# Two feed-forward networks around an attention layer: last tiles scaled and quantised on other engines, value bias row made from sums

## The chip, the cores and the metric

The kernel runs on one core of one Trainium2 chip. A core has a matmul engine (TensorE, PE in the profile; its weight loads are PEld), VectorE (DVE), ScalarE (ACT), GpSimd (POOL) and SyncE (SP), which here only issues DMAs. They run side by side and wait for one another by semaphores. The metric is the device time of one execution in microseconds; the median of three executions is given. Times within the trace are counted from the span's start.

## The reference

x has 2 sequences of 2048 rows of 256 values, 4096 rows in all. Cut to what matters:

```python
x = x + 0.5 * ffn(layernorm(x), w_gate, w_up, w_down)
x = x + attn(layernorm(x), Wq, bq, Wk, bk, Wv, bv, Wo, bo)   # biases bq, bk, bv, bo
x = x + 0.5 * ffn(layernorm(x), w_gate, w_up, w_down)

def fp4_quant_dequant(x):          # blocks of 16 values along a row
    scale = max(max(abs(xb)) / 6.0, 1e-12)
    q = GRID[searchsorted(MID, abs(xb / scale))] * sign(xb / scale) * scale
def fp4_linear(x, w): return fp4_quant_dequant(x) @ fp4_quant_dequant(w).T
def ffn(x, w_gate, w_up, w_down):  # 256 -> 704 -> 256
    h = silu(fp4_linear(x, w_gate)) * fp4_linear(x, w_up)
    return fp4_linear(h, w_down)
def attn(x, ...):                  # one head over all 2048 rows of a sequence
    w = softmax((qr @ kr.T + qi @ ki.T) / sqrt(256))
    return interleave(w @ vr, w @ vi) @ Wo.T + bo
```

## The kernel before, in words

The 4096 rows are 32 tiles of 128 rows, numbered 0 to 31 (NT is 32). Each network goes over the tiles in steps; f is 0 for the first network and 1 for the second. Every engine has its own program, written out by hand, and its order is the order of the code: within a queue nothing overtakes. All matmuls of the networks are done in halves of precision, an upper part (T_hi, w_hi) and a lower part (T_lo, w_lo), so that three products make one.

What happens to the hidden values of a tile k, in order:
- TensorE makes gate and up products into `gu` (a PSUM region); ScalarE applies silu; VectorE multiplies to `z` (L854).
- VectorE takes the maximum of each block (`amax`, L867), and the scales `s_up`, `s_neg` and their inverse `s_inv` (to L880). `z` times `s_inv` is `y` (L908 on VectorE, L607 on GpSimd); ScalarE makes the absolute values (L1495, for the last tile L1486); VectorE rounds to the grid in two operations (`rounded` L889, `grid` L895); grid times `s_neg` is `zq` (L625 on GpSimd, 704 columns and then 64; for the last two tiles L974 and L976 on VectorE).
- TensorE transposes `zq` into PSUM (L1887, six or eight passes). ScalarE copies the upper part `T_hi` (L1513; for the last two tiles in two pieces, L1519 and L1520). The lower part comes from VectorE by a subtraction (L950), for tile 29 from a product with the negative identity on TensorE (`chain_lower`, L2045) and a copy by ScalarE (`T_lo`, L1527), for the last two from VectorE (L960 to L966).
- TensorE projects down into the one bank `dn` (ten passes of L2017 and seven of L2024; for the last two tiles L2172 and L2181; tile 31 has a bank of its own, `dn_last`). ScalarE copies `dn` out to `down` (`down_out`, L1502), and GpSimd adds that to `x` (`residual`, L592). TensorE may start the next tile's projection only when the copy is done: it waits for `down_done`.

In step c the engines work at tiles c-1 to c+3 at once. The step functions decide by comparisons of c with NT what differs for the last tiles: NT-4 is 28, NT-3 is 29, NT-2 is 30, NT-1 is 31. Tiles 30 and 31 are projected in `last_two`. ScalarE also takes the statistics of finished tiles (`mean_of`, `minus_mean`, `variance_of`; st_junk in the rows) in the first network.

Behind the first network come keys, queries and scores. The bias of keys and values is turned into two rows, `rk_sum` and `bv_sum`, by products of four pieces each (L1894): the bias spread over 128 columns (`bkB`, `bvB`) against `wq_s` and the transposed output weights `woT`. ScalarE copies both rows out (`bias_rows`), GpSimd adds `bo` (`output_bias`), and ScalarE takes the first scores out of PSUM after that. Early in the run, GpSimd makes `wv_d`, differences of the value weights.

## Time and profile before

| | us |
|---|---|
| median of 3 runs | 896.74 (896.65 to 897.13) |
| the profiled execution | 896.82 |
| its span, first to last instruction | 895.0 |
| TensorE busy | 873.4 (98%) |
| VectorE, ScalarE, GpSimd busy | 710.1, 627.5, 566.9 |
| share of the chain that ended last | TensorE 90%, VectorE 3%, ScalarE 3% |

The granted TensorE clock is printed as full throughout. Busy time of a matmul includes its way through the array, so passes overlap in the rows; the distance between two starts is what a pass costs in the queue. The first network ends near 258 us, the attention near 690 us, and the last 15 us are the end of the second network.

### The profile page before, as it was taken

Reading aid. Unit: us, or ns where it says so; the run is one execution under the profiler, and the core shown is the slowest. Engines: PE = TensorE matmul, PEld = TensorE weight load, DVE = VectorE, ACT = ScalarE, POOL = GpSimd, SP = SyncE. Lnnn points to the kernel's source line nnn. Section 1 sums busy time; section 2 is a strip of 40 time slices with the busy share of each in tenths; the row PEclk is TensorE's granted clock in tenths of the full one; section 3 lists DMA queues with packets and bytes.
Section 4 is the critical chain, followed back from the end, with each engine's and each line's share of the span. In section 5 each row is a group of like instructions: output and inputs, shape, how many; then the busy total and the mean of one; then the engine's idle time right before and its main releaser. Section 6 shows DMA issues by size and latency. Waiting matters only on the chain.

```text
span 895.0 us, 14668 instructions
## 1 busy us (share of the span) xinstructions
PE 873.4 (98%) x4842; PEld 754.2 (84%) x4842; DVE 710.1 (79%) x1104; ACT 627.5 (70%) x1395; POOL 566.9 (63%) x636
## 2 busy tenths in 40 slices
PE   4999999999999999999999999999999999999997
PEld 3788999999988788888888788888778999999996
DVE  7987999999977897855656646455688999999997
ACT  6789888977685866758685786758785676555543
POOL 5577889988520554536658454636667778877762
PEclk9999999999999999999999999999999999999999
DMA  9200000000000000000000000000000000000001
GB/s 314 72 1 1 1 1 2 0 2 1 1 1 1 1 1 1 0 1 0 1 1 1 1 1 1 0 1 1 1 1 1 1 25 25 24 25 25 1 25 48
DMA packets 11948, 13.73 MB, mean 15 GB/s; under 512 B 864, under 2 KB 11104, under 8 KB 11872
## 3 DMA queue, kind: packets, MB, share of 16 engines
q1 hardware_dynamic: 11872, 12.79, 4.3%
q8 instruction: 39, 0.64, 0.3%
q14 instruction: 37, 0.30, 0.1%
HBM read 8.59 MB, written 4.19 MB: 14 GB/s over the span
## 4 chain that ended last, share of the span: by engine, by line
PE 90%; DVE 3%; ACT 3%; issue 1%; POOL 1%; DMA 1%; SPq 0%; DVEq 0%; ACTq 0%; POOLq 0%
PE bank L2006 26%; PE bank L2270 19%; PE bank L2333 18%; PE bank_b L2017 7%; PE bank L1887 7%; PE bank_b L2024 5%; PE bank L2260 2%; PE bank L2078 1%; PE bank_b L2078 1%; DMA wk_s<-in_L_attn_Wk 1%; PE bank L1894 1%; PE bank L1883 1%; POOL xt L713 1%; DVE rounded L889 0%; PE bank_b L1894 0%
## 5 line engine op out<-in xcount | busy, mean ns | idle before, releaser
L676 POOL TENSOR_TENSOR p_lo<-s_ring,p_hi 128x512 fp32r<-128x512 f32 x128 | 167.7, 1315 | 187.2 <-ACT p_hi L1725 186.8
L2006 PE MATMUL bank<-w_hi,T_hi 128*128 128x512 f32 (+1 forms) x384 | 149.8, 390 | 0.9 <-DVE s_ring L1096 0.7
L625 POOL TENSOR_TENSOR zq<-grid,s_neg 128x256 f32<-128x256 f32 (+2 forms) x184 | 142.1, 800 | 13.6 <-DVE grid L895 13.6
L2006 PE MATMUL bank<-w_lo,T_hi 128*128 128x512 f32 (+1 forms) x384 | 144.0, 375 | 0.0
L2006 PE MATMUL bank<-w_hi,T_lo 128*128 128x512 f32 (+1 forms) x384 | 144.0, 375 | 0.0
L2333 PE MATMUL bank<-p_hi,xv 128*128 128x512 f32 x512 | 140.8, 393 | 0.0
L1072 DVE TENSOR_TENSOR top<-bank,top 128x512 f32<-128x512 f32 x92 | 63.5, 690 | 93.4 <-ACT s_ring L1708 91.7
L1708 ACT ACTIVATE s_ring<-bank 128x512 f32<-128x512 f32 x128 | 75.8, 593 | 73.3 <-PE bank L2270 66.7
L1513 ACT ACTIVATE T_hi<-bank 128x1024 fp32r<-128x1024 f32 (+1 forms) x68 | 64.7, 951 | 80.1 <-PE bank L1887 80.0
L2333 PEld LDWEIGHTS bank<-p_hi,xv 128*128 128x128 f32 x512 | 94.0, 188 | 18.1 <-DVE p_lo L1054 0.2
L607 POOL TENSOR_TENSOR y<-z,s_inv 128x960 f32<-128x960 f32 (+1 forms) x56 | 99.7, 1781 | 5.4 <-DVE rounded L889 4.6
L2270 PE MATMUL bank<-q_hi,k_hi 128*128 128x512 f32 x256 | 100.6, 393 | 0.5 <-ACT s_ring L1708 0.3
L2270 PE MATMUL bank<-q_hi,k_lo 128*128 128x512 f32 x256 | 99.7, 389 | 0.0
L2270 PE MATMUL bank<-q_lo,k_hi 128*128 128x512 f32 x256 | 99.6, 389 | 0.0
L1714 ACT ACTIVATE s_ring<-s_ring 128x512 f32<-128x512 f32 x128 | 79.2, 622 | 20.5 <-DVE s_ring L1096 20.5
L1096 DVE TENSOR_TENSOR s_ring<-s_ring,bank 128x512 f32<-128x512 f32 x128 | 84.6, 677 | 0.4
L867 DVE TENSOR_REDUCE amax<-z 128x60 f32<-128x960 f32 (+2 forms) x72 | 74.9, 1040 | 11.7 <-ACT z L1547 9.0
L1725 ACT ACTIVATE p_hi<-s_ring 128x512 fp32r<-128x512 f32 x128 | 80.7, 631 | 4.4 <-PE bank L2333 1.2
L2006 PEld LDWEIGHTS bank<-w_hi,T_lo 128*128 128x128 f32 x384 | 72.1, 188 | 11.8
L2006 PEld LDWEIGHTS bank<-w_hi,T_hi 128*128 128x128 f32 x384 | 72.2, 188 | 11.6 <-DVE s_ring L1096 1.1
L2333 PE MATMUL bank<-p_lo,xv 128*128 128x512 f32 x256 | 80.8, 390 | 0.0
L2017 PE MATMUL bank_b<-wd_hl,T_hi 128*128 128x256 f32 x600 | 79.9, 279 | 0.0
(238 smaller groups left out, 1925.4 us busy)
## 6 DMA issues: line engine op xcount, KB each, us to landing
out<-x SPq DMA_DIRECT2D x7, 512.0 KB, 2.9
x<-in_L_attn_hidden_states SPq DMA_DIRECT2D x3, 1024.0 KB, 12.3
x<-in_L_attn_hidden_states SPq DMA_DIRECT2D x2, 512.0 KB, 7.5
wraw<-in_L_ffn_w_down SPq DMA_DIRECT2D x1, 704.0 KB, 7.6
wraw<-in_L_ffn_w_up SPq DMA_DIRECT2D x1, 640.0 KB, 5.4
wq_s<-in_L_attn_Wq SPq DMA_DIRECT2D x1, 512.0 KB, 7.0
wk_s<-in_L_attn_Wk SPq DMA_DIRECT2D x1, 512.0 KB, 7.9
wo_s<-in_L_attn_Wo SPq DMA_DIRECT2D x1, 512.0 KB, 8.4
```

The lines of the kernel that those rows point to most:

```text
L607: nc.gpsimd.tensor_tensor(out=blocks(y[:, lo:Z]), in0=blocks(z[:, lo:Z]), in1=spread(s_inv[:, lo // BLOCK:ZB], (Z - lo) // BLOCK), op=ALU. ...
L625: last = nc.gpsimd.tensor_tensor(out=blocks(zq[:, to:to + hi - lo]), in0=blocks(grid[:, lo:hi]), in1=spread(s_neg[:, par, lo // BLOCK:hi / ...
L676: nc.gpsimd.tensor_tensor(out=lower_buf(n, c), in0=score_buf(n, c), in1=upper_buf(n, c).bitcast(F32), op=ALU.subtract).then_inc(plo_done, 1)
L867: nc.vector.tensor_reduce(out=amax[:, n], in_=blocks(z[:, lo:hi]), axis=AX_X, op=ALU.max, apply_absolute_value=True).then_inc(amax_done, 1)
L1096: nc.vector.tensor_tensor(out=p, in0=p, in1=shift_bank, op=ALU.subtract).then_inc(diff_done, 1)
L1708: nc.scalar.activation(score_buf(n, c), score_bank(c), ACT.Copy).then_inc(evac_done, 1)
L1714: nc.scalar.activation(p, p, ACT.Exp, scale=SCALE).then_inc(exp_done, 1)
L1725: nc.scalar.activation(upper_buf(n, c), score_buf(n, c), ACT.Copy).then_inc(phi_done, 1)
L2006: last = nc.tensor.matmul(gu[:, lo:hi], lhsT=T[:, par, HK + kd, :], rhs=w[:, kd, lo:hi], start=n == 0, stop=n == len(terms) - 1)
L2017: nc.tensor.matmul(dn, lhsT=T_hi[:, par, k, :], rhs=wd_hl[:, k, half:half + D], start=n == 0, stop=False)
L2270: last = nc.tensor.matmul(score_bank(c), lhsT=kk[:, kd, t], rhs=q[:, kd, :], start=kd == 0 and i == 0, stop=kd == KD - 1 and i == 2, skip_ ...
L2333: last = nc.tensor.matmul(sum_bank[:, kd, :], lhsT=xv[:, c, of], rhs=p, start=c == 0 and first == 0, stop=c == CH - 1 and first == 2, skip ...
```

## The change

It reorders the last steps of both networks and makes the value bias row in another way:
- GpSimd scales tile 31 (`scaled_last`, in place in `z`) where VectorE did, and quantises tile 30 where VectorE did. VectorE goes from tile 30's grid straight to tile 31, with other buffers (`gu` for the absolute values, `yabs_sb` for the result, `bank5` for its transposes).
- GpSimd adds tiles 28 and 29 to x only after tile 31 is quantised.
- ScalarE copies tile 28 out of `dn` after the absolute values of tile 31, and tile 29 between the two pieces of tile 30's upper part.
- In the second network TensorE transposes tile 29 between the passes of tile 28; in both, tile 31 between those of tile 30.
- The value bias row: GpSimd multiplies `woT` by the bias and adds the four pieces in two steps; TensorE makes one product with ones, after the first score product. ScalarE copies the key row out in step 30 and the value row later.
- The statistics of tiles 28 and 29 go from the first network to the first rounds of attention.

The core of the diff:

```diff
-        dn_last = bank4[:, 1, 0:D]
+        dn_last = bank4[:, 2, 0:D]
...
-            return bank5[:, 0:2, :] if k == NT - 2 else bank2[:]
+            return bank5[:, 0:2, :] if last(k) else bank2[:]
+
+        def quantised_of(k):
+
+            return yabs_sb if last(k) else zq
...
-                nc.gpsimd.tensor_copy(bkB[:], b3[:, 1, :].unsqueeze(2).to_broadcast([P, KE, P]))
-                nc.gpsimd.tensor_copy(bvB[:],
-                                      b3[:, 2, :].unsqueeze(2).to_broadcast([P, KE, P])).then_inc(aw["bcast"], 1)
+                nc.gpsimd.memset(ones[:], 1.0).then_inc(aw["ones"], 1)
+                nc.gpsimd.tensor_copy(bkB[:],
+                                      b3[:, 1, :].unsqueeze(2).to_broadcast([P, KE, P])).then_inc(aw["bcast"], 1)
+
+            def value_bias_sums():
+
+                pool.wait_ge(aw["nv"], KD)
+                nc.gpsimd.tensor_tensor(out=woT[:], in0=woT[:], in1=b3[:, 2, :].unsqueeze(2).to_broadcast([P, KE, D]),
+                                        op=ALU.mult).then_inc(aw["bv_mul"], 1)
+                pool.wait_ge(aw["bv_mul"], 1)
+                nc.gpsimd.tensor_tensor(out=woT[:, 0:2, :], in0=woT[:, 0:2, :], in1=woT[:, 2:4, :],
+                                        op=ALU.add).then_inc(aw["bv_add"], 1)
+                pool.wait_ge(aw["bv_add"], 1)
+                nc.gpsimd.tensor_tensor(out=woT[:, 0, :], in0=woT[:, 0, :], in1=woT[:, 1, :],
+                                        op=ALU.add).then_inc(aw["bv_sum"], 1)
...
+                def scaled_last():
+
+                    pool.wait_ge(inv_done, number(f, NT - 1))
+                    nc.gpsimd.tensor_tensor(out=blocks(z[:, 0:I]), in0=blocks(z[:, 0:I]), in1=spread(s_inv[:, 0:HB], HB),
+                                            op=ALU.mult).then_inc(y_done, 1)
+
                 def step(c, par):
                     if whole(f, c + 2):
                         pool.wait_ge(inv_done, number(f, c + 2))
                         negative_scales(c + 2, par)
-                    if hidden(c - 1) and c < NT:
+                    if hidden(c - 1) and c < NT - 3:
                         residual(c - 1, 1 - par)
                     if hidden(c + 2) and ahead(c + 2):
                         scaled_by_pool(c + 2)
-                    if chain(c + 1) and not late(c + 1):
+                    if c == NT - 3:
+                        scaled_last()
+                    if chain(c + 1) and not last(c + 1):
                         quantised(c + 1, 1 - par)
+                    if c == NT - 2:
+                        pool.wait_ge(zq_done, number(f, NT - 1))
+                        residual(NT - 4, 0)
+                        residual(NT - 3, 1)
+                    if c == NT - 1:
+                        residual(NT - 2, 0)
...
                     if f == 0 and c == NT:
+                        value_bias_sums()
                         output_bias()
...
-                    abs_k = silu[:] if last(k) else yabs_of(f, k, lo, hi)
+                    abs_k = gu[:, 0:I] if last(k) else yabs_of(f, k, lo, hi)
...
-                        scaled(NT - 1)
                         to_grid(NT - 2)
-                        quantised_late(NT - 2, 1 - par)
...
-                def quantised_late(k, par):
-
+                def quantised_last(par):
+
+                    k = NT - 1
                     dve.wait_ge(grid_done, number(f, k))
-                    dve.wait_ge(T_done, number(f, k - 1))
-                    nc.vector.tensor_tensor(out=blocks(zq[:, 0:I]), in0=blocks(grid[:, 0:I]),
+                    dve.wait_ge(zq_done, number(f, k) - 1)
+                    nc.vector.tensor_tensor(out=blocks(yabs_sb[:, 0:I]), in0=blocks(rounded[:, 0:I]),
                                             in1=spread(s_neg[:, par, 0:HB], HB), op=ALU.mult)
...
                     if late(c) and chain(c):
                         late_upper(c, par)
+                        if c == NT - 2:
+                            down_out(c - 1, 1 - par)
+                        late_upper_rest(c, par)
                     if extra and c == NT - 1:
                         keys_upper(0, 0)
-                    if hidden(c - 1) and c < NT and c != NT - 2:
+                    if hidden(c - 1) and c < NT and c not in (NT - 3, NT - 2):
...
-                    if extra and c == NT - 3:
+                    if c == NT - 3:
                         absolute(NT - 1)
+                        down_out(c - 1, 1 - par)
+                    if extra and c == NT - 2:
+                        key_bias_out()
...
-            bias_rows()
             sum_inputs_upper(0, 0)
+            value_bias_out()
...
-                    if n == 1 and c in (4, 7):
-                        statistics(NT - 2 + (c - 4) // 3, NT - 2 + (c - 4) // 3)
+                    if n == 1 and c in (4, 7, 10, 13):
+                        statistics(NT - 4 + (c - 4) // 3, NT - 4 + (c - 4) // 3)
...
-                product(bv_sum, bvB, woT, False).then_inc(aw["rows"], 1)
+                pe.wait_ge(aw["ones"], 1)
+                pe.wait_ge(aw["bv_sum"], 1)
+                pe.wait_ge(x_last, 1)
+                nc.tensor.matmul(bv_sum, lhsT=ones[:], rhs=woT[:, 0, :], start=True, stop=True,
+                                 skip_group_check=True).then_inc(aw["rows"], 1)
...
-                        project_down_first(par, dn)
-                        wait_lowered(f, c)
+                        if f and c == NT - 4:
+                            project_down_first(par, dn, 0, 2)
+                            wait_lowered(f, c)
+                            transpose_chain(f, c + 1)
+                            project_down_first(par, dn, 2)
+                            chain_lower(f, c + 1, 1 - par)
+                        else:
+                            project_down_first(par, dn)
+                            wait_lowered(f, c)
                         project_down_rest(par, dn)
...
                         transpose_keys(0, 0)
-                    down_late(0, dn)
+                    pe.wait_ge(down_done, (NT - 1) * f + NT - 2)
+                    down_late(0, dn, 0, 2)
                     transpose_chain(f, NT - 1)
+                    down_late(0, dn, 2, HK)
                     down_late_rest(0, dn)
-                    down_late(1, dn_last)
+                    if f == 0:
+                        pe.wait_ge(aw["rows_s"], 1)
+                    down_late(1, dn_last, 0, HK)
                     down_late_rest(1, dn_last)
 
-                def down_late(par, dn):
-
-                    pe.wait_ge(late_hi, 2 * f + par + 1)
-                    if par == 0:
...
             queries(0)
             transpose_keys(0, 1)
+            scores(0, 0)
             value_bias_row()
-            scores(0, 0)
+            scores(0, 1)
             pe.wait_ge(aw["rows_s"], 2)
             transpose_keys(0, 2)
-            scores(0, 1)
             pe.wait_ge(klo_done, 2)
...
```

What the order of instructions shows at three places. First ScalarE in the first network, from step 29 to the statistics behind it; `bank<-y` is absolute values of tile 30, `down` is the copy out of `dn`. Before:

```order
L1495 ACTIVATE bank<-y 128x704
L1502 ACTIVATE down<-bank_b 128x256
L1413 ACTIVATE st_junk,total<-x 128x256
L1513 ACTIVATE T_hi<-bank 128x1024
L1419 ACTIVATE nmean<-total 128x1
L1420 ACTIVATE nmean_s<-total 128x1
L1527 ACTIVATE T_lo<-bank 128x896
L1529 ACTIVATE T_hi<-bank 64x128
L1486 ACTIVATE silu<-z 128x704
L1426 ACTIVATE st_junk,var<-x,nmean_s 128x256
L1447 ACTIVATE xk<-x,nmr,rstd 128x256
L1502 ACTIVATE down<-bank_b 128x256
```

In the changed kernel (its lines are numbered anew: L1539 is `down_out`, L1523 the absolute values of tile 31, L1556 and L1561 the two pieces of the upper part):

```order
L1532 ACTIVATE bank<-y 128x704
L1450 ACTIVATE st_junk,total<-x 128x256
L1550 ACTIVATE T_hi<-bank 128x1024
L1456 ACTIVATE nmean<-total 128x1
L1457 ACTIVATE nmean_s<-total 128x1
L1568 ACTIVATE T_lo<-bank 128x896
L1570 ACTIVATE T_hi<-bank 64x128
L1523 ACTIVATE bank<-z 128x704
L1539 ACTIVATE down<-bank_b 128x256
L1463 ACTIVATE st_junk,var<-x,nmean_s 128x256
L1484 ACTIVATE xk<-x,nmr,rstd 128x256
L1556 ACTIVATE T_hi<-bank 128x512
```

The copy of tile 28 (`down`) moves from the second row to behind `T_lo` and the absolute values of tile 31, and stands in both networks at this place; the copy of tile 29 moves between the pieces of tile 30's upper part.

Then TensorE at the end of the second network, from the down projection of tile 28 on. Before:

```order
L2006 MATMUL bank<-w_hi,T_lo 128x384
L2017 MATMUL bank_b<-wd_hl,T_hi 128x256 x10
L2024 MATMUL bank_b<-wd_hl,T_hi 128x256 x2
L2024 MATMUL bank_b<-wd_hl,T_lo 128x256 x5
L1887 MATMUL bank<-ident,zq 128x128 x6
L2045 MATMUL bank<-T_hi,neg_ident 128x512 x2
L2017 MATMUL bank_b<-wd_hl,T_hi 128x256 x10
L2024 MATMUL bank_b<-wd_hl,T_hi 128x256 x2
L2024 MATMUL bank_b<-wd_hl,T_lo 128x256 x5
L1887 MATMUL bank<-ident,zq 128x128 x6
L2172 MATMUL bank_b<-wd_hl,T_hi 128x256 x10
```

In the changed kernel (L2066 and L2073 are the ten and seven passes, L1932 the transposes, L2094 the product with the negative identity):

```order
L2055 MATMUL bank<-w_hi,T_lo 128x384
L2066 MATMUL bank_b<-wd_hl,T_hi 128x256 x4
L1932 MATMUL bank<-ident,zq 128x128 x6
L2066 MATMUL bank_b<-wd_hl,T_hi 128x256 x6
L2094 MATMUL bank<-T_hi,neg_ident 128x512 x2
L2073 MATMUL bank_b<-wd_hl,T_hi 128x256 x2
L2073 MATMUL bank_b<-wd_hl,T_lo 128x256 x5
L2066 MATMUL bank_b<-wd_hl,T_hi 128x256 x10
L2073 MATMUL bank_b<-wd_hl,T_hi 128x256 x2
L2073 MATMUL bank_b<-wd_hl,T_lo 128x256 x5
L1932 MATMUL bank<-ident,zq 128x128 x6
L2232 MATMUL bank_b<-wd_hl,T_hi 128x256 x4
```

The six transposes of tile 29 and the product behind them move ahead of the end of tile 28, and tile 31's transposes move up into the first passes of tile 30.

Last GpSimd behind the first network. Before, from the quantising of tile 29:

```order
L625 TENSOR_TENSOR zq<-grid,s_neg 128x704
L625 TENSOR_TENSOR zq<-grid,s_neg 128x64
L592 TENSOR_TENSOR x<-x,down 128x256
L529 TENSOR_TENSOR var<-var,eps_all 128x4
L532 TENSOR_TENSOR rstd<-var,mhalf 128x4
L535 TENSOR_TENSOR nmr<-nmean,rstd 128x4
L592 TENSOR_TENSOR x<-x,down 128x256 x2
L585 TENSOR_TENSOR bias_row<-bias_row,bo_row 128x256
```

In the changed kernel, from the same place (L650 is `scaled_last`):

```order
L642 TENSOR_TENSOR zq<-grid,s_neg 128x704
L642 TENSOR_TENSOR zq<-grid,s_neg 128x64
L650 TENSOR_TENSOR z<-z,s_inv 128x704
L642 TENSOR_TENSOR zq<-grid,s_neg 128x704
L642 TENSOR_TENSOR zq<-grid,s_neg 128x64
L609 TENSOR_TENSOR x<-x,down 128x256 x3
L584 TENSOR_TENSOR woT<-woT,b 128x1024
L587 TENSOR_TENSOR woT<-woT 128x512
L590 TENSOR_TENSOR woT<-woT 128x256
L602 TENSOR_TENSOR bias_row<-bias_row,bo_row 128x256
```

GpSimd scales tile 31 and quantises tile 30, adds three tiles one behind another, and makes three operations on `woT` ahead of the bias sum.

## Rows read from the trace of the kernel before

**Rows 1.** TensorE's waits, whole run: us in total, times, longest.
```profile
PE bank L1894 <- DMA wk_s<-in_L_attn_Wk: 12.8, 1, 12.8
PE bank L2045 <- ACT T_hi L1513: 1.1, 1, 1.1
```

**Rows 2.** TensorE timeline, value bias product: start, us, engine, line.
```profile
262.09 1.89 PE L1894 MATMUL bank<-woT,bvB 128*128 128x256 f32 x8
263.63 0.58 PE L2270 MATMUL bank<-q_hi,k_hi 128*128 128x512 f32 x1
```

**Rows 3.** Groups by line and shape, GpSimd: count, busy us, mean ns.
```profile
L676 POOL TENSOR_TENSOR p_lo<-s_ring,p_hi 128x512 fp32r<-128x512 f32 x128 | 167.7, 1315 | 187.2 <-ACT p_hi L1725 186.8
...
L625 POOL TENSOR_TENSOR zq<-grid,s_neg 128x704 f32<-128x704 f32 x60 | 86.1, 1435 | 5.2 <-DVE grid L895 5.2
L592 POOL TENSOR_TENSOR x<-x,down 128x256 f32<-128x256 f32 x62 | 45.9, 741 | 27.8 <-ACT down L1502 23.8
```

**Rows 4.** Timelines of GpSimd and VectorE near 25 us.
```profile
24.58 0.81 POOL L573 COPY bvB<-b 128x512 f32<-128x512 f32 x1
25.35 1.89 POOL L579 TENSOR_TENSOR wv_d<-wv_s 128x1024 f32<-128x1024 f32 x1
...
26.48 0.83 DVE L798 TENSOR_SCALAR wsm<-wsm 128x88 f32<-128x88 f32 x1
```

**Rows 5.** TensorE timeline, end of the first network.
```profile
248.91 1.33 PE L2017 MATMUL bank_b<-wd_hl,T_hi 128*128 128x256 f32 x10
...
258.38 0.50 PE L2260 MATMUL bank<-k_hi,m_hi 128*128 128x512 f32 x1 [0.25 <-DVE k_lo L1031]
```

**Rows 6.** ScalarE timeline, end of the first network.
```profile
246.27 0.38 ACT L1502 ACTIVATE down<-bank_b 128x256 f32<-128x256 f32 x1 [0.66 <-PE bank_b L2024]
...
249.11 0.92 ACT L1527 ACTIVATE T_lo<-bank 128x896 fp32r<-128x896 f32 x1 [0.97 <-PE bank L2045]
...
250.34 0.79 ACT L1486 ACTIVATE silu<-z 128x704 f32<-128x704 f32 x1
251.04 0.49 ACT L1426 ACTIVATE st_junk<-x,nmean_s 128x256 f32<-128x256 f32 x1
```

**Rows 7.** Chain that ended last, 225 to 270 us: start, us, what.
```profile
244.24 1.17 PE bank_b L2017 x10
245.41 0.82 PE bank_b L2024 x7
246.23 0.66 PE bank L1887 x6
...
261.38 0.87 PE bank L1883 x8
```

**Rows 8.** Waits of all engines, 285 to 345 us.
```profile
ACT s_ring L1708 <- PE bank L2270: 10.5, 14, 0.9
```

**Rows 9.** Chain that ended last, second network's end.
```profile
881.10 1.31 DVE z L908
...
887.48 0.89 DVE zq L974
```

**Rows 10.** TensorE timeline, end of the second network.
```profile
878.28 1.33 PE L2017 MATMUL bank_b<-wd_hl,T_hi 128*128 128x256 f32 x10
...
880.26 0.81 PE L1887 MATMUL bank<-ident,zq 128*128 128x128 f32 x6
...
882.76 1.33 PE L2017 MATMUL bank_b<-wd_hl,T_hi 128*128 128x256 f32 x10
...
890.12 1.44 PE L2172 MATMUL bank<-wd_hl,T_hi 128*128 128x256 f32 x10
```

**Rows 11.** ScalarE timeline, end of the second network.
```profile
880.46 0.38 ACT L1502 ACTIVATE down<-bank_b 128x256 f32<-128x256 f32 x1 [1.61 <-PE bank_b L2024]
...
882.96 0.92 ACT L1527 ACTIVATE T_lo<-bank 128x896 fp32r<-128x896 f32 x1 [0.82 <-PE bank L2045]
```

**Rows 12.** Chain that ended last, first passes of the run.
```profile
12.76 3.75 PE bank L1894 x8
```

64 lines of the change are left out of this document (36 added, 28 removed).

## Prediction, made before the changed kernel ran

> **What bounds the kernel now.** I read the page's busy line first (TensorE is busy 873.4 of 895.0 us, in the table above), then TensorE's waits [rows 1]. After the initial wait for a weight DMA of 12.8 us, no wait is longer than the 1.1 us near the very end. So TensorE sets the time nearly everywhere. The change can gain in two ways only: by fewer passes on TensorE, or by closing its small gaps. It can lose wherever it makes TensorE wait. Then I read the timelines of all engines around the two ends of the networks (240 to 270 us, 855 to 895 us) and, because one broadcast on GpSimd goes, around 20 to 42 us. A time of the chain and a time of the timeline can differ by up to 0.2 us for the same instructions, since ends of matmuls are modelled; I count intervals between starts.
>
> **Part 1, the value bias product.** Before, four fp32 products show as eight passes that begin at 262.09, and the next score product begins at 263.63 [rows 2]: 1.54 us. One product of the same width is a quarter, 0.39. Gain 1.15 us. It now needs GpSimd's three sums first. Nearest rows [rows 3, 4]: 1024 elements 1.89 us, 512 elements 1.32, 256 elements 0.74, so 4.0 us in all. They start once GpSimd has added tile 30, which I put at 259.6 (below), and end at 263.6. TensorE comes to the product only after the first score product, near 265.4. The 1.8 us between them is the cover. If it were gone, each microsecond of lateness would cost one, since the next score product is queued behind. The same few queue places move ScalarE's copy of the row behind the 1.06 us copy of xv; I see 0.6 us of room there.
>
> **Part 2, the end of the first network.** The accumulator of the down projection is one bank (dn). TensorE may start tile 29's products only when ScalarE has copied tile 28 out. Before, that copy is at 246.27, long ahead of TensorE's start at 248.91 [rows 5, 6]. The order of ScalarE after the change puts it behind T_lo (249.11), the 64-row remainder and the absolute values of tile 31 (250.34) [rows 6]. None of these can move up: T_lo waits for TensorE's subtraction product, which stands behind the key bias product on TensorE. GpSimd's scaling of tile 31, about 1.45 us by the 704-wide form [rows 3], is done by 248.4 and doesn't count. So the copy takes the place in which a statistic ran, 251.04, and with 0.39 us ends at 251.43. TensorE starts tile 29 at about 251.5 instead of 248.91: **2.6 us late**.
>
> How much comes back? From 248.91 to the query product at 258.38 are 9.47 us. Pure work in it: three times 1.17 and 0.82, two sets of six transposes at 0.66, one set of eight at 0.87 [rows 7], together 8.2. The rest, 1.3 us, are gaps. After the change the gaps left are one of 0.2 (the transposes of tile 30 and of the keys end near 255.05, ScalarE then still finishes the upper part, 0.6, and the copy of tile 29, 0.39, at 255.25) and small hand-overs of 0.3. Start of the query product: 251.5 + 8.2 + 0.5 = 260.2, against 258.38: +1.8. The low part of the keys on VectorE is ready near 259.8, so it is not what is waited for any more. GpSimd's last residual follows the copy of tile 30, near 258.8, and ends at 259.6, as used in part 1.
>
> Around the bias row I add 0.1: the first score product now comes straight after the transposes, and its second half has to wait some 0.2 us for the low part of the queries, which the old bias product covered; one change between kinds of products goes. Parts 1 and 2 together: +1.8 - 1.15 + 0.1 = **+0.7**. From there to the second network TensorE runs without a gap that the change touches. The statistics of tiles 28 and 29 move into the first block of scores, where ScalarE stands up to 0.9 us before each copy of a score bank [rows 8]. I put a tile's statistics at 1.2 us of ScalarE, so two rounds hide one tile; without that cover two tiles would cost 2.4 us.
>
> **Part 3, the end of the second network.** Before, the chain runs through VectorE, which scales tile 31 from 881.10 and quantises it until 888.5 [rows 9]. After: scaling goes to GpSimd (881.1 to 882.55), VectorE goes straight on with tile 30's grid (to 882.95), GpSimd quantises tile 30 by about 884.75 (1.44 and a remainder of 0.3), and VectorE is through with tile 31 near 886.35: 2.15 us sooner. But TensorE doesn't get that. Its first four passes of tile 28 start at 878.28, the transposes of 29 then at 878.75 instead of 880.26 [rows 10]. T_lo followed those transposes by 2.70 (882.96) [rows 11], so it starts at 881.45. The absolute values follow 1.23 later as in the first network, at 882.7, the copy of tile 28 0.7 after them at 883.4 [rows 6], and it ends at 883.8. It was at 880.46 before [rows 11]. TensorE has finished tile 28 at 882.05 and stands until 883.8. Tile 29 then starts at 883.85 instead of 882.76 [rows 10]. Tile 29's passes end at 885.85, the transposes of 30 at 886.5; the upper part of 30 and the copy of 29 (0.6 and 0.39) end at 887.6. Four passes 0.5, transposes 0.66, six passes 0.7, seven 0.85: the last group of ten starts at 890.3. Before: 890.12 [rows 10]. So **+0.2**: the gap at tile 30's transposes is closed, and the same time is lost at the bank.
>
> **Part 4, the start.** GpSimd drops a 0.81 us copy and sets ones instead (at most 0.2), so wv_d begins 0.6 sooner [rows 4]. This matters because VectorE's small operation L798, 0.83 us long, ends at 27.31 just when wv_d ends at 27.24 [rows 4]; an operation of a tenth of the elements of the others shouldn't take that long. It seems held by GpSimd, and it lies on the chain that leads to a short gap of TensorE near 36.5. Gain between 0 and 0.5; since the copy of bk now meets another VectorE operation, I take **-0.2**. The Trainium skill's page "SBUF — State Buffer", section "Who interferes with whom", says that VectorE in a two-port mode and GpSimd exclude each other for a whole instruction. By that rule the hold moves with wv_d's end and the gain is near 0.3; by the row alone, without a mechanism, it is 0 and the sum 0.2 higher.
>
> **Sum.** +0.7 + 0.2 - 0.2 = +0.7. The profiled execution of before took 896.82 us (span 895.0 and 1.8 around it), 0.08 above the median of 896.74. So 897.5 for such an execution, and **897.4** for a median.
>
> **Rivals.**
> Stalls at the bank don't bind (faster). If the copy of tile 28 came in time in both networks, the first end would save 1.8 us against my count, and the second 1.9, up to the 2.15 by which VectorE is sooner: 893.7. For it speaks that VectorE was the last chain before [rows 9]. Against it: both orders of ScalarE are fixed, and the copy stands behind two instructions whose inputs are late. It decides if the copy ends before 249 in the first network or before 882 in the second. Only the second of these is thinkable: 895.5. Chance 6%.
> The clock falls in the new gap (slower). After the 12.8 us wait at the start the eight first passes took 3.75 us [rows 12], though eight like them took 1.54 later [rows 2]: that is the level of 1.2 GHz against 2.4. If a gap of 2.6 us is enough, the passes behind it cost about 2.2 us more: 899.6. The longest gap after which this trace shows full speed is 1.1 us [rows 1], so the point from which it decides lies between 1.1 and 12.8. Chance 8%. The Trainium skill's page "TensorE: Matmul & The Clock Gate", section "Part 1: The HAM clock gate (the "warmup" mystery)", tells of a gate that halves the clock when TensorE has been idle; this trace agrees for 12.8 us and doesn't say for 2.6.
> GpSimd's sums come late (slower). If the in-place product with a broadcast operand takes over twice 1.89 us, the cover of 1.8 is gone and the cost is the rest, 0.5 to 2 us: 898 to 899.4. For it: no row has this form in place. Against: wv_d has the same width with a broadcast operand. Chance 6%.
> My forecast, with its sizes: 80%, own range 896.5 to 898.3.
>
> **How the numbers follow.** A measurement of this kernel can tell from no change what is beyond 0.2%, 1.8 us: below 894.9 or above 898.5. Forecast and late sums lie mostly inside. Faster gets the no-stall case and a little of its half: 5%. Slower gets the clock case, part of the late sums and the tail of my sum: 12%. Same: 83%. The range takes in the half case and most of the late sums, from 896.0 to 898.7.
>
> **What would show it.** First network: the copy of tile 28 at about 251 behind the absolute values, tile 29's products at 251.5, a TensorE wait of about 2.5 us on down, the query product near 260. Bias: two passes, 0.4 us, no wait for GpSimd. Second network: a wait of 1.7 us before tile 29's products, VectorE idle before its last lower parts, and an end within 0.5 us of the old one counted from 878.3. Start: L798's follower short, 0.2 us gained by 37. I am wrong if the products of tile 29 start without that wait, if passes behind it last 0.6 instead of 0.38 us, or if the three sums end after 265.

## Result, and the profile after

| | before | changed |
|---|---|---|
| median of 20 executions each | 896.38 us (895.92 to 897.13) | 897.46 us (896.53 to 899.05) |
| ratio, 95% interval | | 1.0013 (1.0007 to 1.0019) |
| profiled execution, its span | 896.82, 895.0 | 897.36, 895.5 |
| TensorE, VectorE, GpSimd busy | 873.4, 710.1, 566.9 | 871.4, 701.6, 575.4 |

The change makes the kernel 0.13% slower: under the 0.2% that the prediction called no change, but more than nothing. The time fell within 0.1 us of the forecast of 897.4. Part of that is luck, as the section on the reasons shows.

TensorE's waits in the changed kernel behind the first DMA (us in total, times, longest), where [rows 1] had nothing over 1.1 us:

```profile
PE bank_b L2066 <- ACT down L1539: 2.3, 1, 2.3
PE bank_b L2066 <- issue: 1.6, 1, 1.6
PE bank_b L2232 <- ACT down L1539: 1.0, 1, 1.0
```

The first row is tile 29 of the first network, the second tile 29 of the second, the third tile 30 of the second. "issue" means that the profile shows nothing that was waited for, but the timeline below does: it is the same copy.

The end of the first network, TensorE's timeline (start, us, engine, line); before: [rows 5].

```profile
246.60 1.89 PE L1939 MATMUL bank<-wq_s,bkB 128*128 128x256 f32 x8
248.14 0.81 PE L2094 MATMUL bank<-T_hi,neg_ident 128*128 128x512 f32 x2
251.29 1.44 PE L2066 MATMUL bank_b<-wd_hl,T_hi 128*128 128x256 f32 x10 [2.35 <-ACT down L1539]
...
252.80 0.75 PE L2073 MATMUL bank_b<-wd_hl,T_lo 128*128 128x256 f32 x5
253.39 0.82 PE L1932 MATMUL bank<-ident,zq 128*128 128x128 f32 x6
...
259.90 0.39 PE L2320 MATMUL bank<-k_hi,m_hi 128*128 128x512 f32 x1
```

ScalarE's timeline at the same place; before: [rows 6].

```profile
248.98 0.92 ACT L1568 ACTIVATE T_lo<-bank 128x896 fp32r<-128x896 f32 x1 [0.98 <-PE bank L2094]
...
250.09 0.74 ACT L1523 ACTIVATE bank<-z 128x704 f32<-128x704 f32 x1
250.86 0.38 ACT L1539 ACTIVATE down<-bank_b 128x256 f32<-128x256 f32 x1
```

Read the two together: `down` ends at 251.24, and the ten passes start at 251.29. The key bias product began at 246.60, 0.12 sooner than before (246.72); the query product begins at 259.90, 1.52 later than before. So this end cost 1.64 us. The last row of TensorE has no wait: the low part of the keys, which TensorE waited for before, is now there in time.

The value bias row: GpSimd's sums, and the product with ones on TensorE; before: [rows 2].

```profile
259.43 1.90 POOL L584 TENSOR_TENSOR woT<-woT,b 128x1024 f32<-128x1024 f32 x1
261.40 1.29 POOL L587 TENSOR_TENSOR woT<-woT 128x512 f32<-128x512 f32 x1
262.78 0.73 POOL L590 TENSOR_TENSOR woT<-woT 128x256 f32<-128x256 f32 x1
```
```profile
265.18 0.59 PE L2013 MATMUL bank<-woT,ones 128*128 128x256 f32 x2
```

The sums end at 263.51, 1.67 before TensorE comes. At the query product the changed kernel is 1.52 late; at the same score products near 268.5 it is 0.41 late. So the value bias row gave 1.11 us. The product itself gave 1.29: its eight passes took 1.54 us before, and the two that are left take 0.25 to the next start. What stands around it took 0.18 back.

The end of the second network, TensorE's timeline; before: [rows 10].

```profile
878.51 0.63 PE L2066 MATMUL bank_b<-wd_hl,T_hi 128*128 128x256 f32 x4
878.99 0.85 PE L1932 MATMUL bank<-ident,zq 128*128 128x128 f32 x6
...
884.08 1.41 PE L2066 MATMUL bank_b<-wd_hl,T_hi 128*128 128x256 f32 x10 [1.58 <-issue]
...
886.15 0.82 PE L1932 MATMUL bank<-ident,zq 128*128 128x128 f32 x6
887.92 0.73 PE L2232 MATMUL bank_b<-wd_hl,T_hi 128*128 128x256 f32 x4 [0.96 <-ACT down L1539]
...
890.67 1.33 PE L2232 MATMUL bank<-wd_hl,T_hi 128*128 128x256 f32 x10
```

ScalarE's copy of tile 28 at the same place:

```profile
883.60 0.39 ACT L1539 ACTIVATE down<-bank_b 128x256 f32<-128x256 f32 x1
```

From the first passes of tile 28 to the last group of ten are 12.16 us; before 11.84. So 0.32 us were lost, although the transposes of tile 29 came 1.50 us sooner, counted from the same first passes.

The start: VectorE's and GpSimd's timelines near 25 us; before: [rows 4].

```profile
26.90 0.25 DVE L831 TENSOR_SCALAR wsm<-wsm 128x88 f32<-128x88 f32 x1
```
```profile
25.02 2.07 POOL L596 TENSOR_TENSOR wv_d<-wv_s 128x1024 f32<-128x1024 f32 x1
```

The small operation that took 0.83 us takes 0.25. Counted against before, TensorE's timeline is 0.32 to 0.36 us late from 20 to 29 us (the first weights landed 0.14 later in this execution) and some 0.15 early from 37 us on, so about 0.5 us came back there.

### The profile page after: what moved, and what is told of

The parts are those of the page before. It is cut to its first block, busy times and chain, and to the rows that moved or that the text cites. A ratio compares the mean times of both kernels' runs of the same rounds, so it can differ in the third digit from the quotient of the medians.

```text
span 895.5 us, 14659 instructions
## 1 busy us (share of the span) xinstructions
PE 871.4 (97%) x4836; PEld 752.9 (84%) x4836; DVE 701.6 (78%) x1098; ACT 626.8 (70%) x1395; POOL 575.4 (64%) x645
## 4 chain that ended last, share of the span: by engine, by line
PE 94%; DVE 2%; ACT 1%; issue 1%; DMA 1%; SPq 0%; POOL 0%; DVEq 0%; POOLq 0%; ACTq 0%
PE bank L2055 27%; PE bank L2330 20%; PE bank L2393 18%; PE bank_b L2066 8%; PE bank L1932 7%; PE bank_b L2073 5%; PE bank L2320 2%; PE bank L2127 1%; PE bank_b L2127 1%; DMA wk_s<-in_L_attn_Wk 1%; PE bank L1928 1%; PE bank L1939 1%; ACT s_ring L1759 0%; PE bank_b L1932 0%; PE bank L2094 0%
## 5 line engine op out<-in xcount | busy, mean ns | idle before, releaser
L642 POOL TENSOR_TENSOR zq<-grid,s_neg 128x64 f32<-128x64 f32 (+2 forms) x188 | 145.3, 800 | 14.3 <-DVE grid L929 14.3
L2066 PE MATMUL bank_b<-wd_hl,T_hi 128*128 128x256 f32 x600 | 80.4, 280 | 3.9 <-ACT down L1539 2.3
L2066 PEld LDWEIGHTS bank_b<-wd_hl,T_hi 128*128 128x128 f32 x600 | 77.5, 188 | 4.5 <-ACT down L1539 2.8
```

Source lines behind the costliest of these rows:

```text
L642: last = nc.gpsimd.tensor_tensor(out=blocks(zq[:, to:to + hi - lo]), in0=blocks(grid[:, lo:hi]), in1=spread(s_neg[:, par, lo // BLOCK:hi / ...
L2066: nc.tensor.matmul(dn, lhsT=T_hi[:, par, k, :], rhs=wd_hl[:, k, half:half + D], start=k == 0 and half == 0, stop=False)
```

## Experiments

Twelve kernels, in four groups. An expectation names its theories by letters, and the text behind it says which of them the run bears out. "Before" stands for the kernel before, run on the same chip in the same group (each group had another chip); it had medians of 896.45 (group of the first four), 896.42 (the next four), 896.82 (the next three) and 897.12 us (the last). Ratios are against it.

### e1_first, e2_second, e3_both: the place of one copy

The copy of tile 28 out of `dn`: in the first network back to its old place (e1), in the second one place up, ahead of the absolute values of tile 31 (e2), or both (e3). Nothing else of the change is touched.

```diff
-                    if hidden(c - 1) and c < NT and c not in (NT - 3, NT - 2):
+                    if hidden(c - 1) and c < NT and c != NT - 2 and (f == 0 or c != NT - 3):
                         down_out(c - 1, 1 - par)
...
                     if c == NT - 3:
+                        if f:
+                            down_out(c - 1, 1 - par)
                         absolute(NT - 1)
-                        down_out(c - 1, 1 - par)
```

(This is e3; e1 has only the effect for f = 0, e2 only that for f = 1.)

Expected of e1_first: 

> The changed kernel, with ScalarE's copy of tile 28 at its old place in the first network only (ahead of the upper part of tile 29). Theory A (the late copy holds the one bank, and TensorE's 2.35 us wait in the first network is real cost): the wait goes, tile 29's products start near 248.9, the query product near 258.2 instead of 259.9; the other waits that come back, tile 31's quantising among them, keep some 0.2 us. Time 1.4 to 1.9 us below the changed kernel, 895.6 to 896.1, about 0.6 us below the kernel before. Theory B (the wait only takes the place of VectorE's or the key chain's, which would be next): less than 0.5 us below the changed kernel, above 897.0.

Expected of e2_second: 

> The changed kernel, with the copy of tile 28 ahead of the absolute values of tile 31 in the second network only. It can't go to its old place there, since the end of tile 28's products now stands behind tile 29's upper part in the queue. Theory A: the copy starts at 882.85 instead of 883.60, tile 29's products at 883.35, and all of it reaches the end: 0.7 us less, 896.8. VectorE gets the absolute values 0.3 us later, which costs nothing, since tile 31 is quantised 1.9 us before its transposes. Theory B (VectorE's chain is what the end hangs on, so a later tile 31 costs): no change or up to 0.3 us more, 897.5 to 897.8.

Expected of e3_both: 

> Both edits of the two runs before. Theory A: the two ends are 600 us apart and their gains add, 2.1 to 2.6 us below the changed kernel: 894.9 to 895.4, faster than the kernel before by 1.0 to 1.5 us. Theory B: within 0.5 us of the changed kernel, not below the kernel before.

Measured: e1 895.35 us (11 executions, ratio 0.9993, 0.9984 to 1.0002); e2 897.52 (0.9999 to 1.0018); e3 894.40, ratio 0.9979 (0.9970 to 0.9988). TensorE in e3, first network:

```profile
246.67 1.89 PE L1940 MATMUL bank<-wq_s,bkB 128*128 128x256 f32 x8
248.85 1.33 PE L2067 MATMUL bank_b<-wd_hl,T_hi 128*128 128x256 f32 x10
...
258.20 0.39 PE L2321 MATMUL bank<-k_hi,m_hi 128*128 128x512 f32 x1
```

There is no wait at tile 29, and from the key bias product to the query product are 11.53 us, against 13.30 in the changed kernel and 11.66 before. The whole loss of the first network hangs on the place of this one copy of 0.38 us. In e3's second network the same distance as above is 11.51 instead of 12.16:

```profile
876.84 0.63 PE L2067 MATMUL bank_b<-wd_hl,T_hi 128*128 128x256 f32 x4
...
888.35 1.33 PE L2233 MATMUL bank<-wd_hl,T_hi 128*128 128x256 f32 x10
```

Two results didn't fit. e1 gained 2.1 us by the median, more than the 1.76 that its trace shows for this end. And e2, whose trace has 11.53 us from tile 28's first passes to the last ten instead of 12.16, didn't become faster by the median. The single times tell why. e2's are 895.97, 896.17, 896.34, 896.38, 896.51, and then 897.52 to 898.19 for the other six: two groups with nothing between them. The changed kernel has, less clearly apart, 12 from 896.53 to 897.68 and 8 from 897.92 to 899.05; e1 has 8 up to 895.75 and 3 from 896.77. e3 has one group, all within 1.04 us. A median over two groups says little.

The record has one more number for every execution, TensorE's granted clock averaged over the whole of it. It is 0.998 in five of e2's upper six (not in the one of 897.67), in all three upper ones of e1, and in eight of the changed kernel's twenty: 897.68 and seven of the eight above 897.9. It is 1.0 in all of e3. Taken at 1.0 alone, the medians are 895.31 (e1), 896.36 (e2) and 897.32 us (changed), and both edits gain: 2.0 and 1.0 us. What the 0.998 means is seen in e7_start.

### e4_bias_only: the value bias row alone

The kernel before with the new value bias row and ones in place of `bvB`; the ends of both networks stay as before.

```diff
-                product(bv_sum, bvB, woT, False).then_inc(aw["rows"], 1)
+                nc.tensor.matmul(bv_sum, lhsT=ones[:], rhs=woT[:, 0, :], start=True, stop=True,
+                                 skip_group_check=True).then_inc(aw["rows"], 1)
```

Expected: 

> The kernel before, with the value bias row alone made the new way (GpSimd's three operations on woT behind tile 30's residual, one product with ones behind the first score product, the key row copied out in step 30). Theory A (TensorE's six passes fewer are gained whole, since GpSimd's sums are hidden): tile 30's residual ends at 258.1, the sums at 262.1, TensorE comes at 263.7: 1.1 us less from here, and 0.1 to 0.2 more from the earlier wv_d at the start, 895.1 to 895.3 against a before of 896.4. Rival (the sums or the later copy of the row hold up scores): a TensorE wait on woT or on the row, and 896 or more.

Measured 894.92 us (894.65 to 895.72), ratio 0.9983 (0.9974 to 0.9992): 1.5 us faster. In its trace the sums run from 257.53 to 261.6, and the product with ones is at 263.24, with no wait. With 1.1 for the product as above, 0.4 is left, near what the changed kernel gained at the start. So the bias row was worth what was forecast, and the ends took it back.

### e5_earlier: the copy still further up

e3 with the second network's copy ahead of `T_lo` of tile 29 too.

```diff
+                    if f and c == NT - 3:
+                        down_out(c - 1, 1 - par)
                     if by_product(f, c):
                         chain_rest(c, par)
                     if c == NT - 3:
-                        if f:
-                            down_out(c - 1, 1 - par)
                         absolute(NT - 1)
```

Expected: 

> The kernel with both copies of tile 28 mended, and in the second network the copy goes one place further up, ahead of T_lo of tile 29. In the trace of the kernel with both mended, tile 28's last passes end near 4.0 us after the network's last group of first passes began, T_lo then occupies ScalarE until 4.4, the copy ends at 4.8, and tile 29 begins 4.92 after. Theory A (ScalarE's order sets tile 29's start): tile 29 begins near 4.5 after, 0.4 sooner; T_lo ends 0.4 later, which is 0.3 before TensorE reaches the products with it, so nothing is given back, and the last group of ten passes begins near 11.1 after instead of 11.5. Median 894.0. Theory B (the tiles 30 and 31 of VectorE and GpSimd are the limit once this bank is mended): tile 29 is sooner but the last group of ten passes stays at 11.5, with a new wait at the transposes, median 894.4.

Measured 894.46 us (893.81 to 895.40), ratio 0.9977 (0.9968 to 0.9986): the same as e3. TensorE and VectorE in the second network:

```profile
877.35 0.63 PE L2067 MATMUL bank_b<-wd_hl,T_hi 128*128 128x256 f32 x4
...
881.87 1.41 PE L2067 MATMUL bank_b<-wd_hl,T_hi 128*128 128x256 f32 x10 [0.52 <-issue]
...
886.55 0.87 PE L1933 MATMUL bank<-ident,yabs_sb 128*128 128x128 f32 x6
```
```profile
883.62 0.89 DVE L923 SCALAR_TENSOR_TENSOR y<-bank,z 128x704 f32<-128x704 f32 x1 [1.81 <-ACT bank L1523]
...
886.28 0.22 DVE L1009 TENSOR_TENSOR yabs_sb<-rounded,s_neg 128x64 f32<-128x64 f32 x1
```

Tile 29 begins 4.52 us after the first passes, 0.4 sooner than in e3, as theory A had it. But the last group of ten begins 11.45 after instead of 11.51: theory B. The copy pushes the absolute values of tile 31 back on ScalarE; VectorE stands 1.81 us for them, and tile 31's transposes now start at 886.55, right behind VectorE's 886.50. The limit has gone from the bank to tile 31.

### e6_sums_late: the cover of the sums

Two more GpSimd products (times one) ahead of the three sums.

```diff
+                for n in (1, 2):
+                    nc.gpsimd.tensor_tensor(out=woT[:], in0=woT[:], in1=ones[:, 0:KE].unsqueeze(2).to_broadcast([P, KE, D]),
+                                            op=ALU.mult).then_inc(aw["bv_mul"], 1)
+                    pool.wait_ge(aw["bv_mul"], n)
```

Expected: 

> The changed kernel with two more GpSimd products over all of woT (times one) ahead of the three operations of the value bias row, to use up their cover. Each is 1.9 us, so the sums end near 267.4 instead of 263.5, while TensorE reaches the product with ones at 265.2. Theory A (cover of 1.7 us, beyond it each microsecond costs one): TensorE waits 2.1 us on woT, time 2.1 us longer than the changed kernel, 899.6. Theory B (there is further slack behind it, since ScalarE copies the score banks and the next products may be waited for anyway): wait seen, but under 1 us of it in the time, 897.9 to 898.4.

Measured 899.51 us (899.06 to 901.02, 5 executions), ratio 1.0036 (1.0024 to 1.0049). The added pair and the product:

```profile
258.89 3.87 POOL L585 TENSOR_TENSOR woT<-woT,ones 128x1024 f32<-128x1024 f32 x2
```
```profile
267.05 0.67 PE L2017 MATMUL bank<-woT,ones 128*128 128x256 f32 x2 [2.27 <-issue]
```

TensorE waits 2.27 us, and the kernel takes 2.05 us more than the changed one (2.10 where only executions with a mean clock of 1.0 are taken, four of its five): theory A. The 1.67 us were all the cover there was, and behind them each microsecond costs one.

### e7_start: GpSimd's load near 25 us

The copy of the key bias is made twice, so that GpSimd has as many 512-element copies there as before.

```diff
-                nc.gpsimd.tensor_copy(bkB[:],
-                                      b3[:, 1, :].unsqueeze(2).to_broadcast([P, KE, P])).then_inc(aw["bcast"], 1)
+                for n in (1, 2):
+                    nc.gpsimd.tensor_copy(bkB[:],
+                                          b3[:, 1, :].unsqueeze(2).to_broadcast([P, KE, P])).then_inc(aw["bcast"], 1)
+                    pool.wait_ge(aw["bcast"], n)
```

Expected: 

> The changed kernel with the copy of the key bias over 128 columns made twice near 24 us, so that GpSimd does there what it did before (two copies of 512 elements) and wv_d begins 0.6 to 0.7 us later, near 25.7. Theory A (VectorE's small operation behind the long reduction is held until wv_d ends): L831 takes 0.8 us or more again, up to wv_d's end near 27.7, and TensorE loses the 0.3 to 0.5 us that the changed kernel had gained by 37 us. Median 897.8. Theory B (its 0.83 us had another cause): L831 takes 0.25 us and nothing moves, median 897.5. A difference of 0.3 us can hardly be seen in the medians; the times within the trace decide.

Measured 898.28 us (897.30 to 898.84), ratio 1.0019 (1.0010 to 1.0028). VectorE and GpSimd:

```profile
26.17 0.95 DVE L833 TENSOR_SCALAR wsm<-wsm 128x88 f32<-128x88 f32 x1
```
```profile
25.16 1.90 POOL L598 TENSOR_TENSOR wv_d<-wv_s 128x1024 f32<-128x1024 f32 x1
```

The hold is back: 0.95 us instead of 0.25, ending at 27.12, `wv_d` at 27.06. And TensorE, 0.73 us ahead of the changed kernel's timeline at 24.5 us, is 0.16 ahead at 42: 0.57 lost. Theory A. (The medians at a mean clock of 1.0, 897.61 against 897.32, differ by 0.3, on different chips.) As a control, e6's timeline was 0.61 ahead at 24.5 and 0.62 at 40. The rule of the Trainium skill's page "SBUF — State Buffer", section "Who interferes with whom" (one of the two engines waits out the other's whole instruction), agrees with where the operation ends. The page ties it to a two-port mode of VectorE, and no row here shows the mode.

The same trace showed more than it was made for. At the end of the first network, TensorE waits 2.35 us as in the changed kernel, but what follows takes longer:

```profile
251.18 2.13 PE L2068 MATMUL bank_b<-wd_hl,T_hi 128*128 128x256 f32 x10 [2.35 <-ACT down L1541]
253.11 0.63 PE L2075 MATMUL bank_b<-wd_hl,T_hi 128*128 128x256 f32 x2
253.54 1.27 PE L2075 MATMUL bank_b<-wd_hl,T_lo 128*128 128x256 f32 x5
254.60 1.05 PE L1934 MATMUL bank<-ident,zq 128*128 128x128 f32 x6
```

Windows of the same trace (stretch, us, busy time and count of PE, PEld, DVE, ACT, POOL, then the granted clock, DMA share, GB/s):

```profile
247.00:250.00 3.00, 1.83 (x9) 1.24 (x7) 1.25 (x2) 2.00 (x6) 2.72 (x3) 1.00 0.00 0
250.00:252.00 2.00, 0.82 (x5) 0.82 (x6) 1.15 (x2) 1.98 (x6) 0.00 (x1) 0.92 0.00 0
252.00:253.00 1.00, 1.00 (x7) 1.00 (x6) 0.97 (x2) 0.11 (x1) 0.00 (x0) 0.50 0.00 0
253.00:254.00 1.00, 1.00 (x7) 1.00 (x7) 0.70 (x2) 0.00 (x0) 0.22 (x1) 0.50 0.00 0
254.00:255.00 1.00, 1.00 (x6) 1.00 (x6) 0.00 (x0) 0.00 (x0) 0.52 (x1) 0.50 0.00 0
```

and of the changed kernel's:

```profile
252.00:253.00 1.00, 1.00 (x11) 1.00 (x10) 0.97 (x2) 0.23 (x1) 0.00 (x0) 1.00 0.00 0
```

Seven passes in a microsecond instead of eleven, at a granted clock of 0.50: the level of 1.2 GHz against 2.4. From 251.18 to the transposes of tile 30 are 3.42 us, against 2.10; by the next down projection 1.57 us are lost. This is the rival "the clock falls in the new gap", and it happens in one execution and not in another of the same gap. The page's digits of the clock in 40 slices don't show it, since 3 us are a small part of a slice. The mean over the execution does: half the clock for some 3.4 us of 897 is 0.998. So the 0.998 of an execution stands for one such fall, and e7 has it in 6 of 11. The reverse isn't safe: the profiled executions of e3 and e5 hold no record of the clock at all, and are printed as 1.0. The few high times at 1.0 (897.67 in e2, 897.92 in the changed kernel, 898.19 in e7, 898.06 in e10) may be such executions; that isn't shown.

### e8_later: a longer gap in the first network

The copy of tile 28 behind the statistic and the normalising of keys as well.

```diff
                     if c == NT - 3:
                         absolute(NT - 1)
-                        down_out(c - 1, 1 - par)
+                        if f:
+                            down_out(c - 1, 1 - par)
...
                         keys_normalised(c - 14)
+                    if extra and c == NT - 3:
+                        down_out(c - 1, 1 - par)
```

Expected: 

> The changed kernel with the first network's copy of tile 28 put still later on ScalarE, behind the statistic and the normalising of keys that follow it (251.14 to 252.22 in the changed kernel's trace). Theory A (each microsecond by which this copy is late costs one; the clock stays): the copy is at 251.95 instead of 250.86, TensorE's wait grows from 2.35 to 3.4 us, the query product is 1.1 us later, median 898.5. Theory B (later work hides a part of it, as 0.8 of 2.4 was absorbed in the changed kernel): under 0.5 us. Theory C (the clock falls in a gap of 3.4 us): the ten passes of tile 29 take over 1.6 us instead of 1.17, and the time is over 900.

Measured 899.13 us (898.09 to 900.59, 7 executions), ratio 1.0029 (1.0018 to 1.0040).

```profile
251.74 1.48 PE L2069 MATMUL bank_b<-wd_hl,T_hi 128*128 128x256 f32 x10 [3.46 <-ACT down L1539]
253.01 0.63 PE L2076 MATMUL bank_b<-wd_hl,T_hi 128*128 128x256 f32 x2
253.44 1.27 PE L2076 MATMUL bank_b<-wd_hl,T_lo 128*128 128x256 f32 x5
```

```profile
253.00:254.00 1.00, 1.00 (x7) 1.00 (x6) 0.14 (x2) 0.00 (x0) 0.73 (x1) 0.50 0.00 0
```

The gap is 3.46 us and tile 29 starts 1.14 us later after the key bias product than in the changed kernel: theory A for the wait. But the query product is 2.47 us later, not 1.1. The clock falls again, this time only after the ten passes (the windows show 0.50 from 253 to 256), and costs 1.33. So theory C holds too, though not with its signs: the ten passes are near their full speed, those behind them are slow, and the time stays under 900. Five of the seven executions have a mean clock under 1.0, and the slowest of them, 900.59, has 0.996, twice the loss of one fall.

### e9_between, e10_filled, e11_filled_second: the gap as the cause

e9: the copy ahead of the absolute values of tile 31 in both networks, which shortens both gaps.

```diff
                     if c == NT - 3:
-                        absolute(NT - 1)
                         down_out(c - 1, 1 - par)
+                        absolute(NT - 1)
```

e10: the changed kernel, TensorE makes idle passes in the first network's gap. e11: e1, with 9 such passes in the second network's gap.

```diff
+                        if f == 0 and c == NT - 3:
+                            for _ in range(18):
+                                nc.tensor.matmul(bv_sum, lhsT=neg_ident[:], rhs=wd_hl[:, 0, 0:D], start=False, stop=True,
+                                                 skip_group_check=True)
                         if f or c:
                             pe.wait_ge(down_done, (NT - 1) * f + c)
```

Expected of e9_between: 

> The changed kernel with the copy of tile 28 ahead of the absolute values of tile 31 in both networks, so still behind T_lo and its remainder. By the traces TensorE's gap in the first network becomes 1.6 us instead of 2.35, and that in the second 0.9 instead of 1.6. The profile of the start experiment showed something that was not in the changed kernel's own profile: behind the same gap of 2.35 us the granted clock stood at 0.50 for some 3 us, and TensorE was 1.45 us later for it. The times of single executions of the changed kernel (20 of them) lie in two groups, 12 from 896.5 to 897.7 and 8 from 897.9 to 899.1. Theory A (in a part of the executions the clock falls behind the gap, the rarer the shorter the gap): the lower group lies near 895.8 (0.75 for the first gap and 0.6 for the second less than 897.2), and fewer executions than 8 in 20 are a microsecond or more above it. Theory B (the two groups have nothing to do with the gap): as many as before lie in the upper group, as before with gaps of at most 1.1 us would then show them too.

Expected of e10_filled: 

> The changed kernel in which TensorE makes 18 passes of 256 columns, whose result nobody reads, in the first network ahead of its wait for the copy of tile 28. They take 2.1 us by the distance of such passes (1.17 for ten), so they lie within the gap of 2.35 us and delay nothing by themselves. Theory A (the upper group of times is the clock that falls behind this gap): the upper group is gone or nearly so, all executions lie within about 1.3 us as those of before do, median 897.0 to 897.2, and the clock is full throughout. Theory B (only the wait matters, or the groups come from elsewhere, such as the gap of 1.6 us in the second network): two groups as before, median 897.4 or more, or some executions left above 897.9.

Expected of e11_filled_second: 

> The kernel with the first network's copy at its old place, in which TensorE makes 9 passes of 256 columns, whose result nobody reads, in the second network ahead of its wait for tile 28's copy (gap of 1.58 us, 1.05 us of passes). Without them 8 of its 11 executions lay between 894.9 and 895.8 and 3 between 896.8 and 897.3. Theory A (the clock also falls at times behind the gap of 1.6 us, and costs 1.5): no execution above 896.3, median 895.2. Theory B (these three have another cause, for instance the 1.0 us wait behind): about 3 in 11 still stand 1.5 us above the others.

(The diff is e10's. The passes of e11 also wait until `gu` has been read.)

Measured, 11 executions each: e9 896.03 us (895.81 to 896.80), ratio 0.9994 (0.9986 to 1.0003); e10 897.36 (896.75 to 898.76), 1.0008 (0.9999 to 1.0017); e11 895.74 (895.03 to 896.38), 0.9990 (0.9981 to 0.9998).

TensorE in e10:

```profile
248.56 2.31 PE L2194 MATMUL bank<-wd_hl,neg_ident 128*128 128x256 f32 x18
251.07 1.43 PE L2066 MATMUL bank_b<-wd_hl,T_hi 128*128 128x256 f32 x10 [0.20 <-ACT down L1539]
```

e9's gaps are 1.70 and 0.93 us, all its executions lie within 1 us, and all have a mean clock of 1.0. e11 too has 1.0 in all 11, where e1 had 0.998 in 3 of 11. Its median of 895.74 is above the 895.2 that was expected, because before too was slower in this group: e11 is 1.08 us below it, e1 at a mean clock of 1.0 was 1.14 below. e10 still has 3 of 11 above 898, two of them at 0.998, which is theory B as its text put it: the first gap is filled, the second of 1.57 us is not, and e1, which has only that gap, had 3 of 11. Put together by gap:

| gaps of TensorE | kernels | executions with a mean clock under 1.0 |
|---|---|---|
| first network 3.46, second 1.58 | e8 | 5 of 7 |
| first 2.35, second 0.93 | e2 | 5 of 11 |
| first 2.35, second 1.58 | changed, e7 | 8 of 20, 6 of 11 |
| first 2.35, then 2.27 at the bias row, second 1.58 | e6 | 1 of 5 |
| second 1.58 alone | e1, e10 | 3 of 11, 2 of 11 |
| first 1.70, second 0.93 | e9 | 0 of 11 |
| at most 1.1, or filled | e3, e4, e5, e11 | 0 of 44 |
| at most 1.1 | before, in the four groups | 0 of 98 |

The last two rows against the others tie the falls to the gaps. Between single rows 11 executions decide little: 3 against 0, as for e1 and e11, can be chance, and so can 5 of 22 behind 1.58 us against 0 of 11 behind 1.70.

### e12_longer_second: the same in the second network

e1 with one more copy of 704 elements on ScalarE ahead of the second network's copy of tile 28; its result isn't used.

```diff
                         if f:
+                            nc.scalar.activation(silu[:], z[:, 0:I], ACT.Abs, scale=ROUND)
                             down_out(c - 1, 1 - par)
```

Expected: 

> The kernel with the first network's copy at its old place, and in the second network one more copy of 704 elements on ScalarE, whose result nobody reads, between the absolute values of tile 31 and the copy of tile 28. The gap of TensorE there grows by 0.75 us, from 1.58 to 2.3, as long as the one that the changed kernel has in the first network. Theory A (in a part of the executions the clock falls behind such a gap, about half of them at 2.3 us, wherever it is): a lower group of executions near 896.0, which is 0.75 above the 895.3 without the added copy, and at least 4 of some 11 executions 1.2 to 1.8 us above that; if the profiled one is among these, its granted clock is 0.5 for some microseconds behind 884. Theory B (the second network's end doesn't react this way, because its gap stands 0.4 us behind another wait and few passes follow): one group near 896.0.

Measured 897.66 us (896.79 to 898.43, 11 executions), ratio 1.0005 (0.9996 to 1.0014). TensorE and a window of its trace:

```profile
882.91 2.47 PE L2068 MATMUL bank_b<-wd_hl,T_hi 128*128 128x256 f32 x10 [2.38 <-issue]
885.18 0.63 PE L2075 MATMUL bank_b<-wd_hl,T_hi 128*128 128x256 f32 x2
```
```profile
883.00:884.00 1.00, 1.00 (x5) 1.00 (x6) 0.97 (x2) 0.00 (x0) 0.00 (x0) 0.50 0.00 0
```

The gap is 2.38 us and the clock is at 0.50 from 883 to 886. From the ten passes to the transposes of tile 30 are 3.55 us instead of 2.08 (e11): 1.47 lost. This is theory A in that the clock falls behind such a gap in this network too. Its share isn't the half that was expected: ten of the eleven executions have a mean clock of 0.998 (897.27 to 898.43), and the one at 1.0 took 896.79. That one is where the lower group was expected, 896.0 and the 0.7 us by which the kernel before was slower on this chip. Two gaps of one length, 2.35 and 2.38 us, at different places and on different chips had the fall in 19 of 42 executions (changed, e2, e7) and in 10 of 11. So the length alone doesn't set how often it comes; what else does wasn't tested.

## Why the prediction came out as it did

**Value bias row, -1.15 and 0.1 around it.** Right: -1.11 in the trace for both, made of 1.29 gained by the product and 0.18 lost around it. The sums end at 263.51 (predicted 263.6), TensorE comes at 265.18 (265.4); e6 shows that the cover ends where it was put.

**First network, +1.8.** Right in mechanism and nearly in size. The copy stands at 250.86 instead of 251.04, tile 29 at 251.29 instead of 251.5, the query product at 259.90 instead of 260.2 (this execution is 0.12 early by then); +1.64. e3 shows that the copy's place is the whole of it: back at its old place the end is 1.77 us shorter.

**Second network, +0.2.** Right: +0.32. The copy begins at 883.60 (predicted 883.4), tile 29 at 884.08 (883.85), the last ten at 890.67 (890.3); this execution is 0.23 late from the first passes of tile 28 on. That VectorE is sooner isn't used, as said; e2 and e3 show 0.63 and 0.65 us to be had if the copy goes ahead of the absolute values, and e5 shows VectorE's tile 31 as the next limit.

**Start, -0.2.** The mechanism was right and the size too small: 0.5 us, the end of the range given for it. e7 takes it back by restoring the hold. This is the term that was mis-sized most. In the changed kernel too the small operation ends (27.15) right behind `wv_d` (27.09), as the prediction's rule for the hold says.

**The clock.** Here the prediction's step failed in its form; the forecast of 897.4 left it out, with a chance of 8%. It asked whether "a gap of 2.6 us is enough", with one point from which it decides, and 2.2 us for all executions. The runs show no such point between yes and no: behind the gap of 2.35 us the clock falls in some of the executions (8 of 20 of the changed kernel), behind 1.58 in the second network in 5 of 22, behind 2.38 there in 10 of 11. What a fall costs is 1.3 to 1.6 us by the traces of e7, e8 and e12, where the prediction took 2.2 from the first passes of the run. Those passes show the slow level by their pace alone: the view of the granted clock prints 1.00 there, because this trace's record of the clock begins at 17.75 us, behind them. The profiled execution of the changed kernel is one where the clock stayed full, so its profile alone would have buried this rival. In the 20 times the falls lift the mean (897.69) above the median at a mean clock of 1.0 (897.32) by 0.4 us, and the median by 0.15.

**The sum.** The terms as measured are -0.5, +1.64, -1.11 and +0.32, +0.35 together, where +0.7 was forecast. The changed kernel's profiled execution was 0.36 us late by 20 us for weights and what follows them, and gained 0.2 between 430 and 495 us: +0.51, against 0.54 between the two profiled executions. Most of that 0.2 is one wait of TensorE for a score copy that the trace of before has and that of the changed kernel has not:

```profile
491.35 0.47 PE L2270 MATMUL bank<-q_hi,k_hi 128*128 128x512 f32 x1 [0.28 <-ACT s_ring L1708]
```

e9's trace has the same wait (0.35), so it isn't shown to be an effect of the change. Median against median the change is +1.08. Two misses cancel in the agreement at 897.4: the three executions given of before had a median 0.36 us above that of the 20, and the change cost 0.4 more than the forecast sum. The falls of the clock in part of the executions give 0.15 of the difference. Against the before of their own groups the same terms give e3 -2.07 (measured -2.05), e4 -1.6 (-1.53), e5 -2.1 (-1.96), and, at a mean clock of 1.0, e1 -1.4 (-1.14) and e2 -0.3 (-0.09). For the changed kernel +0.35 stands against +0.9 at a mean clock of 1.0. So 0.5 to 0.6 us of its median stay open, half of the measured +1.08: the traced terms account for the two profiled executions, but not for the whole distance of the medians. Falls of the clock that the record misses could be behind a part of it; no trace here shows one.

**The other rivals.** Stalls that don't bind: not so, both copies are waited for. Late sums: not so, 1.90 us for the in-place product, as its nearest row said; e6 shows what they would have cost.

## What to carry to other kernels

A small instruction that frees a bank belongs ahead of everything in its queue whose input comes late; one copy of 0.38 us, moved behind two instructions whose inputs come late, took back more (1.77) than the fewer matmul passes had brought (1.11). Of the changes tried, the value bias row alone (e4, 894.92) or the whole change with the copies put back (e3, 894.40) is what to keep. When the single times of a kernel fall into two groups, read the mean granted clock of each execution, look for a pause of TensorE of some 2 us, and compare executions at the same clock only. One profile can miss the fall. To test a pause, fill it with unused passes (e10, e11) or shorten it (e9), and run enough executions to tell 3 of 11 from none.
